# Two transformer layers on one core: loads reordered, weight rounding cut in quarters, table loads placed by hand, last norm and gate curves moved

## The reference, cut to what matters

```
mod = (silu(c) @ wmod).reshape(2, 6, 1, 512);  sa, ca, ga, sb, cb, gb = mod[:, 0..5]
ga, gb = sign * max(|.|, 0.25)
h = layernorm(x) * (1 + ca) + sa;   x = x + ga * attn(h)
h = layernorm(x) * (1 + cb) + sb;   x = x + gb * ffn(h)
```

## Time and profile before

| | us |
|---|---|
| median of three runs | 918.02 |
| the profiled execution | 918.86 |
| its span, first to last instruction | 917.1 |
| PE busy | 859.0 (94%) |
| DVE busy | 678.6 (74%) |
| ACT busy | 532.4 (58%) |
| POOL busy | 192.2 (21%) |

### The profile page before, as it was taken

How to read it: one execution, slowest core, us unless ns; L and a number is a source line. 1 busy time by engine, 2 the same in 40 slices (tenths; PEclk the granted TensorE clock), 3 DMA queues, 4 the chain that set the end, 5 groups by cost and what they waited for, 6 DMA issues and landing times.

```text
span 917.1 us, 13670 instructions
## 1 busy us (share of the span) xinstructions
PE 859.0 (94%) x5096; PEld 678.0 (74%) x5096; DVE 678.6 (74%) x1066; ACT 532.4 (58%) x707; POOL 192.2 (21%) x199
## 2 busy tenths in 40 slices
PE   3698999999889998998999999999988999999998
PEld 1466777777667776787878888788877888888886
DVE  3745888889888788697777787577886866667852
ACT  2412667777563643766566667577647766666840
POOL 3002576667837043000000000000120000000004
PEclk9798999999999999999999999999999999999999
DMA  8588478887733032124333334133302433332202
GB/s 296 192 255 165 52 103 136 132 120 110 127 106 104 35 81 69 46 70 134 90 90 103 104 100 132 31 112 93 115 26 68 136 92 93 103 105 68 70 1 92
DMA packets 38450, 95.35 MB, mean 104 GB/s; under 512 B 7144, under 2 KB 10216, under 8 KB 37360
## 3 DMA queue, kind: packets, MB, share of 16 engines
q1 hardware_dynamic: 34256, 89.11, 39.9%
q10 hardware_dynamic: 4128, 5.36, 1.7%
HBM read 79.56 MB, written 2.21 MB: 89 GB/s over the span
## 4 chain that ended last, share of the span: by engine, by line
PE 53%; DVE 9%; DMA 5%; ACT 4%; issue 3%; SPq 1%; POOL 0%; POOLq 0%; DVEq 0%; ACTq 0%
PE PS L1614 10%; PE PS L1615 10%; PE PS L1616 10%; PE PS L1927 5%; PE PS L1928 5%; PE PS L1926 5%; DMA WF<-in_LBGU 4%; SPq L525 1%; DVE WF L1241 1%; DVE ACC L1233 1%; DVE WRL L1245 1%; PE PS L1658 1%; DMA WOF<-in_WO 1%; PE PS L1911 1%; ACT PT L951 1%
## 5 line engine op out<-in xcount | busy, mean ns | idle before, releaser
L903 ACT ACTIVATE PL<-CODE 128x1024 f32<-128x1024 int32 x200 | 202.3, 1056 | 58.3 <-DVE ACC L1233 55.6
L1614 PE MATMUL PS<-HH,WRH 128*128 128x512 f32 x448 | 177.4, 396 | 10.0 <-DVE HID L1556 6.7
L1616 PE MATMUL PS<-HL,WRH 128*128 128x512 f32 x448 | 176.3, 393 | 0.0
L1615 PE MATMUL PS<-HH,WRL 128*128 128x512 f32 x448 | 176.2, 393 | 0.0
L780 POOL TENSOR_TENSOR X<-X,SCR 128x512 f32<-128x512 f32 x32 | 42.4, 1330 | 554.9 <-DVE SCR L1218 554.4
L1233 DVE SCALAR_TENSOR_TENSOR ACC<-PL,ACC 128x1024 f32<-128x1024 f32 x100 | 123.5, 1235 | 9.4 <-DVE ACC L1233 1.4
L951 ACT ACTIVATE PT<-PS 128x512 f32<-128x512 f32 x160 | 86.3, 603 | 45.2 <-PE PS L1735 22.4
L797 POOL TENSOR_TENSOR QS<-ident,MX 64x256 fp32r<-64x256 f32 x128 | 98.1, 766 | 57.3 <-DVE MX L1392 36.5
L1614 PEld LDWEIGHTS PS<-HH,WRH 128*128 128x128 f32 x448 | 85.3, 190 | 31.0 <-issue 11.5
L1616 PEld LDWEIGHTS PS<-HL,WRH 128*128 128x128 f32 x448 | 85.1, 190 | 18.2
L1615 PEld LDWEIGHTS PS<-HH,WRL 128*128 128x128 f32 x448 | 85.4, 191 | 17.0
(11 more groups left out here) (230 smaller groups left out, 1506.7 us busy)
## 6 DMA issues: line engine op xcount, KB each, us to landing
CODE<-in_CODES SPq DMA_DIRECT2D x50, 512.0 KB, 3.5
SCALE<-in_SCALES SPq DMA_DIRECT2D x100, 256.0 KB, 4.0
WM<-in_WM SPq DMA_DIRECT2D x12, 1024.0 KB, 5.2
QS<-FQ SPq DMA_DIRECT2D x32, 256.0 KB, 6.4
X<-in_X ACTq DMA_DIRECT2D x2, 1024.0 KB, 12.5
KS<-KHL SPq DMA_DIRECT2D x32, 64.0 KB, 5.3
KN<-KHL SPq DMA_DIRECT2D x32, 64.0 KB, 4.3
GAB<-gates SPq DMA_DIRECT2D x4, 512.0 KB, 3.6
```

What stands on the lines that cost most here:

```text
L903: nc.scalar.activation(PL[:, n % 3], CODE[:, p % 2], ACT.Prelu, scale=scale, bias=bias, alpha=alpha).then_inc(s_plane, 1)
L1614: nc.tensor.matmul(dst, lh, rh, start=start and k == 0, stop=False)
L1615: nc.tensor.matmul(dst, ll, rh, start=False, stop=False)
L1616: ins = nc.tensor.matmul(dst, lh, rl, start=False, stop=stop and k == KC - 1)
```

## The change

It has six parts.

1. **Loads.** ACT issues ident, X of batch 0 and the constants. SP issues CT, WM 0 and 1, WQ, X of batch 1, WM 2, WK and WV and the other WM; it no longer waits for WQ. On DVE the XN of batch 0 stand ahead of the modulation columns, and the low part of WQ is made in two halves, one ahead of the first HL, one (with WK/WV) behind the last; PE waits for the first half at the first query product and for the second at the third.
2. **Output weight.** WOH is rounded in quarters, behind units 59 to 62, where it was one instruction behind unit 58. Two of the head splits are moved two units on (51 to 53, 59 to 61).
3. **Table loads.** `prepare` issues an activation of one column with the function needed next, behind the last use of the former one.
4. **Experts.** `LAG` is 5, with a fifth tile ZT4; the decode steps 6 and 7 stand behind tiles 3 and 4, one each.
5. **Last norm.** The transposes of `norm(3, 0)` stand ahead of the last down tile of n = 0, with semaphores of their own (s_n3, s_h3), and the DVE work around them is in a new order: the decode sums of the next piece are spread among the SCR, the split of piece 30 and the scale of piece 31 too.
6. **Gate curves and finish.** For n = 0, SG of batch 0 stands ahead of the low-rank rounding and of WRH and fold. For n = 1 and the first three pieces, curves, sums and finish stand behind SG and HID of their place.

The core of the diff:

```diff
-LAG = 4
+LAG = 5
-SPLIT_AT = {46: 0, 51: 1, 54: 2, 59: 3}
+SPLIT_AT = {46: 0, 53: 1, 54: 2, 61: 3}
 # SP
                         sp.dma_start(WQKVF[:, :, 0:D], a["WQ"]...).then_inc(s_wq, 16)
-                        sp.wait_ge(s_wq, 16)
+                        load_tokens(sp, 1)
+                    if n == len(FIRST) + 1:
+                        sp.dma_start(WQKVF[:, :, D:D + KVW], a["WK"]...).then_inc(s_wkv, 16)
+                        sp.dma_start(WQKVF[:, :, D + KVW:], a["WV"]...).then_inc(s_wkv, 16)
 # ACT
+            def prepare(i, function):
+                nc.scalar.activation(WARM[:, i:i + 1], ident[:, 0:1], function)
...
+            prepare(0, ACT.Exp)    # behind the SD of norm 0; then Sqrt, Exp, Sqrt, Silu, Sqrt, Silu
...
-                if n == units - 6:
-                    act.wait_ge(s_wo, 16 * REP)
-                    act.wait_ge(s_used, len(CAPS) * N_QKV)
-                    nc.scalar.activation(WOH[:], WOF[:], ACT.Copy).then_inc(s_w0h, 1)
+                if units - 5 <= n < units - 1:
+                    c = n - (units - 5)
+                    if c == 0:
+                        act.wait_ge(s_wo, 16 * REP)
+                        act.wait_ge(s_used, len(CAPS) * N_QKV)
+                    ins = nc.scalar.activation(WOH[:, c], WOF[:, c], ACT.Copy)
+                    if c == KC - 1:
+                        ins.then_inc(s_w0h, 1)
...
-                if t < NT // 2:
-                    for i in (2 * t, 2 * t + 1):
-                        decode_step(*o_step(i))
+                for i in ((0, 1), (2, 3), (4, 5), (6,), (7,), (), (), ())[t]:
+                    decode_step(*o_step(i))
...
-                    if curves_of is not None:
+                    ahead = n == 1 and m < RING
+                    if curves_of is not None and not ahead:
                         all_curves(GU_START[n] + AHEAD + curves_of)
-                    if n == 0 and b == 0:
-                        round_low_rank(GU0 + AHEAD + m + 1)
...
                     nc.scalar.activation(SG[:, i % 2], ..., ACT.Silu).then_inc(s_sg, 1)
+                    if ahead and curves_of is not None:
+                        all_curves(GU_START[n] + AHEAD + curves_of)
+                    if n == 0 and b == 0:
+                        round_low_rank(GU0 + AHEAD + m + 1)
+                    if (n == 0 or ahead) and finish_of is not None:
+                        finish(GU_START[n] + AHEAD + finish_of)
 # DVE
+            def split_projections(part):
+                nc.vector.tensor_tensor(WQKVL[:, :, part], WQKVF[:, :, part], WQKVH[:, :, part], ALU.subtract
+                                        ).then_inc(s_wqkvl, 1)
...
+                normalise(0, b)
                 if b == 0:
                     for j in FIRST:
                         mod_column(0, j)
-                normalise(0, b)
-                if b == 0:
+                    dve.wait_ge(s_wqkvh, 1)
+                    split_projections(slice(0, D // 2))
                     modulate(0, 0)
+                    split_projections(slice(D // 2, D))
+                    dve.wait_ge(s_wqkvh, 2)
+                    split_projections(slice(D, D + 2 * KVW))
...
                 if n == 0:
+                    curve_sum(p, 0); curve_sum(p, 1)
+                    gated(("down", n, 0)); curve_sum(p, 2); gated(("down", n, 1)); added_stats(0)
+                    split_piece(p - 1)
+                    gated(("down", n, 2)); added_stats(1); gated(("down", n, 3)); added_stats(2)
+                    gated(("down", n, 4)); added_stats(3)
                     normalise(3, 0)
+                    scale_piece(p)
+                    gated(("down", n, 5)); gated(("down", n, 6))
                     modulate(3, 0)
+                    gated(("down", n, 7))
+                    for t in range(TB, NT): added_stats(t)
                     normalise(3, 1)
 # PE
+                    if key == ("q", 0, REP // 2):
+                        pe.wait_ge(s_wqkvl, 2)
...
-                if n == 0:
-                    norm(3, 0)
+                    if (n, t) == (0, NT - 2):
+                        norm(3, 0)
```

122 lines of the change are left out of this document (83 added, 39 removed).

## The result

The changed kernel takes 902.98 us (901.53 to 903.28, four runs) against 917.42 (916.58 to 918.38, four runs) for the kernel before: ratio 0.983, 95% interval 0.9811 to 0.9849, so 14.4 us less. The two profiled executions lie further apart, 918.86 and 901.53, spans 917.1 and 899.7: 17.4.

What follows compares the result with a forecast made beforehand. PE, busy 94% of the span, was taken to bound the kernel. A 4.6, B 0.35, C 2.9, D 2.5, F 7.4 and H to J 1.0 sum to 18.75 us off the median 918.02, giving 899.2; range 892.5 to 907.

Steps and rivals of the forecast that it cites:

- D: Experts: LAG 5 and the later decode steps take 2.5 us off PE's waits of 4.3; ends 1.0 and 4.6.
- A: Start: half split of WQ, earlier XN and reordered loads bring 4.6 us; low end 3.0, high end 5.3.
- B: Attention: the head split moved from unit 51 to 53 brings 0.35 us (0 to 0.8).
- C: End of attention: output weight in quarters and the other moved split bring 2.9 us; ends 1.0 and 4.2.
- F: Gate/up n = 0: first stall gone and periods down from 11.85 to PE's 11.38, 7.4 us; ends 2.0 and 7.6.
- slice by slice: Start, low end: 0.5 us taken off for a first product that waits for its input slice by slice.
- The hold: End of attention: POOL's ATL still holds DVE's FQ, which stays over 3 us, leaving 2.9 of 3.5 us.
- table loads elsewhere: Table loads other than those at 426.14 and 689.22: they end in waits of ACT anyway, so 0.
- R1: Rival, gate/up n = 0: the load loop still sets the pace, periods stay 11.85, total 904.7; chance 0.20.
- H to J: Last norm and gate/up n = 1: waits for HL and HID covered, a new one for WRL; 1.0 us, ends -1.5 and +4.
- The 1.1 set aside for piece 32: Gate/up n = 1: 1.1 us taken off because piece 32 is decoded behind 31 with 2 us less time.
- the signs that were named: Marks expected in the trace, among them first product at 25.2 to 26.9, FQ beside ATL over 3 us, HL waits under 1.

Runs made afterwards that it cites:

- experiment 5: Changed kernel with loads issued as in the kernel before (both batches, WK and WV by ACT; SP waits for WQ): 903.34 us, ratio 0.9817.
- experiment 8: Changed kernel with the first query product of batch 0 waiting for HL slice by slice instead of for the fourth: 898.51 us, ratio 0.9772.
- experiment 6: Changed kernel with WOH rounded whole behind unit 58, head splits at their new units: 906.60 us, ratio 0.985.
- experiment 2: Changed kernel with the experts' last two decode steps back behind one tile (tile 3), LAG still 5: 904.35 us, ratio 0.9861.
- experiment 1: Changed kernel with LAG back at 4, fold steps left at their new places: 905.53 us, ratio 0.9867.
- experiments 10 and 11: Changed kernel, BTL in quarters: plus ATL behind POOL's first additions, 900.63 us; plus edits of experiment 8, experiment 9 and experiment 3 and POOL reordering, 892.37 us.
- experiment 3: Changed kernel without the early activation that loads the silu table ahead of norm 2: 901.51 us, ratio 0.983.
- experiment 9: Changed kernel with piece 31's rounding right behind batch 0's last norm rounding, its split later, batch 1's norm rounding ahead of the curves: 898.13 us, ratio 0.977.
- experiment 12: Changed kernel with curves, sums and finish of gate/up n = 1 back ahead of SG and HID for the first three pieces: 901.19 us, ratio 0.9805.

## Why the prediction was right or wrong

It said 899.2 in 892.5 to 907.0. The time lies in the range and the direction is right; the gain is 14.4 where 18.8 were forecast. By the profiles it is 17.4 against 18.75. Three of the missing four lie in which executions were profiled. That the profiles come so near the sum is in part luck: D was too high by 1.8 and norm 2, counted as nothing, lost 1.2, while A, B with C, and F were too low by 2.0 together.

- **A, start: 4.6; measured 5.5**, and 4.7 with the mean start of experiment 5. The split came out near what was said: 3.7 for the order on DVE (2.28 + 1.26 = 3.5 forecast) and about 1 for the loads (1.1), the latter within the scatter. One reading was wrong: WQ was issued behind the first two modulation weights in the kernel before too; what left their way is X of batch 1 and ACT's issues of WK and WV. The "slice by slice" of the low end doesn't hold for this product, which waited for the fourth HL; experiment 8 shows that this was worth 2.4.
- **B and C, attention: 3.25; measured 4.0** (9.5 less 5.5). The quarters are worth 3.6 (experiment 6). Two things stand behind the size. The slow stretch behind the wait of 3.87 (256.20 to 259.60) was left out of the price: with the wait and it gone, the matmul that stood at 259.08 comes 12.0 earlier, 6.7 more than the one at 88.41. Then 1.1 of it is given back by 267, and 1.5 more at the output product, where ATL's hold makes PE wait 2.11 for 0.63. The hold was foreseen, but on FQ: it fell on NUM, and FQ took 0.69.
- **D, experts: 2.5; measured 0.7. This is the term that missed**, with its neighbour "table loads elsewhere: 0". The moved fold did its part (2.08 to 0.25 ahead of the fifth y product; experiment 2 loses 1.5 without it). `LAG` 5 did not: it took 1.2 off the first wait and put a new one of 1.64 ahead of the fourth y product. That is the longer chain of zt, FH, FL and y, which the prediction named and priced, with all else, at 4.3 - 2.5 = 1.8. 

  The other miss is the table load, which held the gate back just there. The exponentials of the gate end 9.3 us earlier than before, but a table load of 1.28 and its activation now stand on ACT between them and BTH, BTL starts only 7.7 earlier, and DVE's SC isn't done until 0.5 us behind it. The gate is held back by 1.5, just what experiment 1 has more in its first wait than the kernel before (3.09 for 1.58). So the 2.4 that experiment 1 gives to `LAG` 5 is for the most part the hiding of this delay. With the load elsewhere and `LAG` at 4 the waits would be about 1.58 + 0.28 + 0.50 + 0.65 = 3.0 where they are 3.5 now: an estimate from rows of two traces, which no run tried. In the changed kernel only 0.5 to 0.6 of the delay is left, which experiments 10 and 11 get back by quarters of BTL. That the load causes the 1.5 is read from the two timelines. The next load, ahead of norm 2, was tried: it costs 1.1 (experiment 3), and is why the lead falls from 10.2 to 9.0.
- **F, gate/up n = 0: 7.4; measured 7.7** (9.0 to 16.7), periods 11.38. The split holds too: the period with the stall was 16.26 (419.88 to 436.14), 4.9 more than 11.38, where 4.6 was said, and the rest gave 2.8. One point failed: the table load, which I made part of the 3.0, needed no new place (experiment 3). The case of the loop (R1) is excluded by the periods, though its total, 904.7, lies nearer to the measured time than the forecast. That total was itself too high: 4.6 less 0.47 in four or five periods is 2.7 to 2.3 and not 2.0.
- **H to J: 1.0; measured 0.7**, and 1.6 or more in eight of the nine traces named in experiment 9. The wait for WRL(31) was foreseen at 3.8 (the working gives 3.7) and is 2.63, at 673.05. The 1.1 set aside for piece 32 went to HL of batch 1. Experiment 9 shows that both were a matter of order on ACT, and experiment 12 that SG's new place gave nothing.

Of the signs that were named, three did not come as said: the first product began at 24.32, ahead of 25.2; FQ was not the one beside ATL; and HL waits stayed under 1 us for batch 0 but not for batch 1 (1.64).

The port rule of the Trainium skill (SBUF — State Buffer, "Who interferes with whom") was borne out: NUM, two SBUF inputs, takes 4.76 us beside a whole ATL, 1.46 beside quarters and 0.69 without. The drain of 1.38 us that the Trainium skill (ScalarE: Activation LUTs, "What ACT_TABLE_LOAD costs") adds to a load does not show: in the profile after, 360.41 + 1.28 is followed by the next activation within 0.02.

## What to carry to other kernels

- An engine that "waits anyway" is no place for a new instruction if its wait ends on time: look at what stands directly behind the wait. One table load moved into such a place cost 1.1 us; another held the gate back by 1.5, of which the fifth z product hid all but some 0.5.
- When a wait shrinks, look whether it is the same wait. Work pulled ahead to cover one wait (the fifth z product, 1.2 us) pushed back the chain behind it and opened another (1.64 us).
- When an in-order engine stands for a transfer, put behind it only what needs the transfer; one short instruction moved ahead of such a wait (SG) was worth 6.5 us over ten periods.
- Before freeing an operation from a neighbour on another engine, follow what is queued behind that neighbour, and what it will run beside next: ATL cost NUM 4 us, then the additions, then XN.
